# Dividing the second head's exponentials of each pair on GpSimd instead of VectorE

## The chip, the cores and the metric

The kernel runs on one core of a Trainium2 chip, with inputs and output in the chip's main memory. The metric is the device time of one execution in microseconds (us). Before the change it is 2291.26 us, the median of 3 runs (2284.45 to 2292.47).

## The reference

The input x is 4 x 1024 x 1024 in fp32. It is normalised, and two branches are computed from it: attention with 16 heads of 64 columns in 4 groups that share keys and values, with a sliding window of 512 and 4 sink positions, and a small network on the last row of each batch whose result is gated with the input.

```python
xn = _layernorm(x, axis=-1)
# attention
att = jnp.einsum('bkgqd,bkjd->bkgqj', q, k) * scale
att = jnp.where(mask[None, None, None, :, :], att, -jnp.inf)
att = jax.nn.softmax(att, axis=-1)
y = jnp.einsum('bkgqj,bkjd->bkgqd', att, v)
s = y @ Wo.T
# network: thought from the last row, 4 steps of a layer norm and a gelu network
out = x + sigmoid(x @ gate_w + gate_b) * broadcast
g = _silu(layer_norm(out, out_gamma, out_beta))
return x + s * g
```

What matters here is the softmax: the exponentials of a row of scores are divided by their sum before they are multiplied with the values. All products run in fp32, the larger ones as sums of high and low parts.

## The kernel before

The program has two parts. `attend` makes the projections and the attention of all four batches, and stores y to memory; `finish` makes the gate, the output projection and the final norm, tile by tile. The change touches `attend` alone.

`attend` goes through 4 batches of 32 steps. A step s is one unit u = 32 b + s: one group of 4 heads (s // 8) and one block of 128 queries (qb = s % 8). A unit looks at 1 to 5 blocks of 128 keys, and for qb above 4 at 4 sink columns too, so a row of `probs` is 128, 256, 384, 512, 640 or 644 columns wide. Of the 32 units of a batch, 12 have 644 columns. `probs` has 8 slots: 4 heads of this unit and 4 of the one before.

Every engine has its order written out by hand in its own `step(b, s)`; semaphores tie them together.

- TensorE makes the scores of heads 0 and 1 (L1010), then the first two transpositions of unit u - 1's probabilities (`turn_probs`, L1039, four heads of one key block at a time), then whatever the step holds of other work: a tile of the next batch turned (L928), rows of the small network (L858), then the scores of heads 2 and 3, further transpositions, pieces of the projections (L973), and last the product with the values (`values`, L1075) of unit u - 1, sinks last. `turn_probs(u, 0)` waits until all four heads are divided.
- VectorE adds the mask and finds the maximum, one head at a time (L1286), splits projections and turned tiles in high and low parts (L1258, L1274), adds the network's sums (L1346). At the end of a step it takes the reciprocal of a pair's two sums (`invert`, L1294), divides these two heads (`divide`, L1303), copies the turned sinks of unit u - 1 (`take_sinks`, L1320), and does the second pair. In steps 21 to 28 of the first three batches it also takes statistics of a tile of the next batch (L86, L90) before the first pair, and normalises the tile (L105) after the second. In steps 26 to 31 of the last batch it splits one or two pieces of the gate's weights there (L1422, two inputs from SBUF). The next step begins with the copy of y (L1310), which TensorE needs before it may use that bank again.
- ScalarE makes the exponentials with their sums (L768) and copies the transpositions from PSUM (L759).
- GpSimd has little to do. In its own loop over the steps it finds 1 / standard deviation of the tile that VectorE has statistics of (`ln_rstd`: an add L96 and a power L98), issues the load of a tile of x (`load_x`, L645, steps 20 to 27 of the first three batches), fills in sink columns of k and v (steps 2, 8 and 27), and for units with sinks packs the divided sink columns of the four heads (`pack_sinks`, L677).
- SyncE issues nearly all other transfers.

The pair's reciprocal is what the divisions wait for:

```python
dve.wait_ge(exp_done, GROUP * u + 2 * pair + 2)
dve.reciprocal(inv_sum[:, part], row_sum[:, part]).then_inc(inv_ready, 1)
```

Of the kernel before, what the change touches and what calls it, by code (L numbers as in the profile page):

```python
# [22 lines left out]
ALU = mybir.AluOpType  # L23
AX = mybir.AxisListType

P = 128
B, T, C = 4, 1024, 1024
HEADS, KV, HS = 16, 4, 64
WINDOW, SINK = 512, 4
HID = 4096  # L30
KB = C // P
TB = T // P
# [11 lines left out]
GROUP = HEADS // KV  # L44
UNITS = KV * TB
# [23 lines left out]
def blocks_of(qb):  # L69

    return min(qb + 1, WB + 1)
# [36 lines left out]
def unit_of(s):  # L108


    return s // TB, s % TB
# [7 lines left out]
def has_sink(qb):  # L119
    return qb > WB  # L120
# [30 lines left out]
def packed_before(u):  # L151

    return (TB - WB - 1) * (u // TB) + max(0, u % TB - WB - 1)
# [12 lines left out]
def attend(nc, shared, y_stored, WT, Y, BC, XS, x, gate_w, Wq, Wk, Wv, in_gamma, in_beta, agg_w, agg_b, pn_gamma, pn_beta, d1_w, d1_b, d2_w, d2_b,  # L166
           bc_w, bc_b):

    with ExitStack() as ctx:
        def sb(name, shape, dt=F32):  # L170
            return ctx.enter_context(nc.sbuf_tensor(name, shape, dt))
# [4 lines left out]
        def sem(name):  # L176
            return ctx.enter_context(nc.semaphore(name))
# [13 lines left out]
        probs = sb("probs", [P, 2 * GROUP, WIDTH])  # L191
# [5 lines left out]
        neg_max, row_sum, inv_sum = (sb(n, [P, 2 * GROUP]) for n in ("neg_max", "row_sum", "inv_sum"))  # L197
# [59 lines left out]
        x_full, x_high, x_taken = sem("x_full"), sem("x_high"), sem("x_taken")  # L257

        scores_ready, masked, exp_done = sem("scores_ready"), sem("masked"), sem("exp_done")
        inv_ready, normed = sem("inv_ready"), sem("normed")  # L260
        turned, pt_ready, pv_done, y_ready = sem("turned"), sem("pt_ready"), sem("pv_done"), sem("y_ready")

        fw_used, rows_ready, f_turned = sem("fw_used"), sem("rows_ready"), sem("f_turned")
# [160 lines left out]
        def v_parts(b, t):  # L424

            return v[:, 0:2 + b % 2:1 + b % 2, t, :, :]
# [9 lines left out]
        with nc.Block() as block:  # L436
# [166 lines left out]
            def _(pool):  # L603
# [60 lines left out]
                def v_sinks(b):  # L664
# [3 lines left out]
                    for head in range(GROUP):  # L668
                        pool.dma_start(v_sink[SINK * head:SINK * head + SINK, :, :].rearrange("p (m g) d -> p m g d", g=2),
                                       v_parts(b, 0)[0:SINK]).then_inc(v_sink_ready, 16)  # L670

                def pack_sinks(u):
                    slots = slice(GROUP * (u % 2), GROUP * (u % 2) + GROUP)
                    pool.wait_ge(normed, GROUP * u + GROUP)
                    if u >= 2:
                        pool.wait_ge(turned, turns_before(u - 1))
                    pool.tensor_copy(sink_cols[u % 2][:, :, :], probs[:, slots, WIDE:WIDE + SINK]  # L677
                                     ).then_inc(sinks_packed, 1)
# [12 lines left out]
                for b in range(B):  # L691
                    for s in range(UNITS):
                        if s == 0 and b:
                            thought_rstd(b)
                        if s == 2:
                            v_sinks(b)
                        if s == 8:
                            k_sinks(b, 1)
                        if b + 1 < B:
                            if s == 27:  # L700
                                k_sinks(b + 1, 0)
                            if 0 <= s - TURN0 + 1 < TB:
                                x_rstd(b + 1, s - TURN0 + 1)
                            if 0 <= s - TURN0 + 2 < TB:
                                load_x(b + 1, s - TURN0 + 2)
                        if has_sink(unit_of(s)[1]):
                            pack_sinks(UNITS * b + s)

# [131 lines left out]
            def _(pe):  # L840
# [180 lines left out]
                def turn_probs(u, i):  # L1021
                    qb = u % TB
                    if i == 0:
                        pe.wait_ge(normed, GROUP * u + GROUP)
                    if turns_before(u) + i >= 2:
                        wait_taken(*(turn_two_ago(u, i)))

                    for step_no in (u, u + 1):
                        item = turned_in(*divmod(step_no, UNITS))
                        if item and (step_no == u or i >= 2):  # L1030
                            pe.wait_ge(x_taken, 2 * turned_no(item) + 2)
                    if i == blocks_of(qb):
                        pe.wait_ge(sinks_packed, packed_before(u) + 1)
                        pe.transpose(t_ps[(turns_before(u) + i) % 2][0:SINKS, 0:P],
                                     sink_cols[u % 2][:, :, :].rearrange("p h k -> p (h k)"), ident[:, :]
                                     ).then_inc(turned, 1)
                        return
                    for head in range(GROUP):
                        last = pe.transpose(t_ps[(turns_before(u) + i) % 2][:, bass.ts(head, P)],  # L1039
                                            probs[:, GROUP * (u % 2) + head, P * i:P * i + P], ident[:, :])  # L1040
                    last.then_inc(turned, 1)
# [146 lines left out]
            def _(dve):  # L1188
# [107 lines left out]
                def divide(b, s, head):  # L1296
                    _, qb = unit_of(s)
                    u = UNITS * b + s
                    width = blocks_of(qb) * P + (SINK if has_sink(qb) else 0)
                    slot = GROUP * (u % 2) + head  # L1300
                    if head % 2 == 0:
                        dve.wait_ge(inv_ready, 2 * u + head // 2 + 1)
                    dve.tensor_scalar(probs[:, slot, 0:width], probs[:, slot, 0:width], inv_sum[:, slot:slot + 1], None,  # L1303
                                      ALU.mult).then_inc(normed, 1)

# [55 lines left out]
                def step(b, s):  # L1361
                    u = UNITS * b + s
                    found = places(b, s)
                    ahead = s - TURN0 + 1 if b + 1 < B and 0 <= s - TURN0 + 1 < TB else None

                    def take_place(i):
                        if found[i] and found[i][4] == STEPS:
                            take_low(*found[i][:3])

                    if u >= 2:  # L1370
                        take_y(u - 2)
                    mask_scores(b, s, 0)
                    mask_scores(b, s, 1)
                    if b and s == 0:
                        if b == 1:
                            dve.wait_ge(bias_loaded, 32)
                        add_rows(b, thought, thought)
                        think(b)
                    if b and s == 1:
                        scale_cols(2, 1 + b)  # L1380
                    if turned_in(b, s):
                        for half in range(2):
                            turned_low(u, turned_in(b, s), half)
                    take_place(0)
                    if b == B - 1 and s == FOLD_AT:
                        add_rows(B, thought, thought)
                        dve.wait_ge(thought_ready, 2 + 2 * B)
                        dve.tensor_copy(t_rows, thought).then_inc(t_rows_ready, 1)
                    if b == B - 1 and s == TURN_AT:
                        dve.wait_ge(f_turned, 2 + B)  # L1390
                        dve.tensor_copy(cols_view[:, 0:KB, :], f_cols.rearrange("p (k b) -> p k b", b=B)
                                        ).then_inc(cols_ready, 1)
                    if b == B - 1 and s == BC_FOLD_AT:
                        dve.wait_ge(bias_loaded, 48)
                        add_rows(1 + B, t_rows, None)
                    if s in HIDDEN_AT[b]:
                        add_hidden(b, HIDDEN_AT[b][s])
                    if TILES_AT[b][s]:
                        add_sums(b, s)
                    mask_scores(b, s, 2)  # L1400
                    mask_scores(b, s, 3)
                    if ahead is not None:
                        stats(b + 1, ahead)
                    invert(b, s, 0)
                    divide(b, s, 0)
                    divide(b, s, 1)
                    take_place(1)
                    if u and has_sink((u - 1) % TB):
                        take_sinks(u - 1)
                    invert(b, s, 1)  # L1410
                    divide(b, s, 2)
                    divide(b, s, 3)
                    if ahead is not None:
                        normalise(b + 1, ahead)
                    if b and s == 0:
                        apply_thought(b)
                    take_place(2)
                    take_place(3)
                    if b == B - 1:
                        for k in GATE_AT.get(s, ()):  # L1420
                            dve.wait_ge(gate_high, k + 1)
                            dve.tensor_tensor(x_lo[:, k, :], xn[k % 2], x_hi[:, k, :].bitcast(F32),  # L1422
                                              ALU.subtract).then_inc(gate_split, 1)
# [393 lines left out]
```

## Time and profile before

| | |
|---|---|
| median of 3 runs | 2291.26 us (2284.45 to 2292.47) |
| the profiled execution, its own time | 2282.0 us |
| its span, first to last instruction | 2280.3 us |
| mean granted TensorE clock | 0.993 |
| busy: TensorE, VectorE, ScalarE, GpSimd | 2207.4, 1456.2, 857.6, 150.6 us |

The attention takes the span to about 1557 us, `finish` the rest. A row of the timeline gives the start in us from the span's start, the duration in us, the engine (PE is TensorE, PEld its weight load, DVE VectorE, ACT ScalarE, POOL GpSimd), the line of the kernel, the operation, what it writes and reads, its shapes and how many instructions are merged in the row; in brackets the idle time before it and what ended it. A row of groups gives the busy time in us, the mean of one in ns, and the idle time before them.

### The profile page before, as it was taken

Reading aid. Unit: us, or ns where it says so; the run is one execution under the profiler, and the core shown is the slowest. Engines: PE = TensorE matmul, PEld = TensorE weight load, DVE = VectorE, ACT = ScalarE, POOL = GpSimd, SP = SyncE. Lnnn points to the kernel's source line nnn. Section 1 sums busy time; section 2 is a strip of 40 time slices with the busy share of each in tenths; the row PEclk is TensorE's granted clock in tenths of the full one; section 3 lists DMA queues with packets and bytes.
Section 4 is the critical chain, followed back from the end, with each engine's and each line's share of the span. In section 5 each row is a group of like instructions: output and inputs, shape, how many; then the busy total and the mean of one; then the engine's idle time right before and its main releaser. Section 6 shows DMA issues by size and latency. Waiting matters only on the chain. (4 is left out here: it accounts for less than half of the span.)

```text
span 2280.3 us, 35897 instructions
## 1 busy us (share of the span) xinstructions
PE 2207.4 (97%) x13577; PEld 1626.1 (71%) x13577; DVE 1456.2 (64%) x3071; ACT 857.6 (38%) x1837; POOL 150.6 (7%) x367
## 2 busy tenths in 40 slices
PE   7999999999999999999999999988999999999998
PEld 6666666766666676666676766656888888888886
DVE  7555567555666746566665556575766776667667
ACT  2354554444454435455443545463111111111111
POOL 2000001000001100000100000000010100100100
PEclk9999999999999999999999999999999999999999
DMA  7586459533447734435863354555243342342431
GB/s 253 176 253 191 139 178 282 188 106 109 157 153 231 244 115 144 160 122 171 276 200 108 117 196 144 211 176 192 93 147 120 119 147 98 141 146 93 147 119 66
DMA packets 173357, 366.53 MB, mean 161 GB/s; under 512 B 12424, under 2 KB 110856, under 8 KB 158880
## 3 DMA queue, kind: packets, MB, share of 16 engines
q1 hardware_dynamic: 168240, 348.30, 45.9%
q0 software_dynamic: 4544, 14.75, 1.9%
q8 instruction: 91, 1.49, 0.3%
q10 hardware_dynamic: 432, 1.57, 0.2%
q14 instruction: 50, 0.41, 0.1%
HBM read 284.79 MB, written 79.72 MB: 160 GB/s over the span
## 5 line engine op out<-in xcount | busy, mean ns | idle before, releaser
L759 ACT ACTIVATE pt<-t_ps 128x512 f32<-128x512 f32 x480 | 265.9, 595 | 533.5 <-PE t_ps L1039 531.8
L973 PE MATMUL j_ps<-x_hi,w 128*128 128x512 f32 x1232 | 413.5, 404 | 0.0
L768 ACT ACTIVATE probs<-probs,neg_max 128x644 f32<-128x644 f32 (+5 forms) x512 | 352.8, 694 | 57.6 <-DVE neg_max L1286 57.4
L1286 DVE CUSTOM_DVE_ANT_0 probs<-s_ps,mask 128x644 f32<-128x644 f32 (+5 forms) x512 | 316.5, 656 | 80.9 <-PE s_ps L1010 76.3
L1672 PE MATMUL out_ps<-wo,w 128*128 128x512 f32 x1536 | 355.1, 390 | 2.7 <-DVE w L1729 2.7
L1672 PEld LDWEIGHTS out_ps<-wo,w 128*128 128x128 f32 x1536 | 289.4, 188 | 63.3 <-issue 3.1
L1672 PE MATMUL gate_ps<-x_hi,w 128*128 128x512 f32 x1024 | 280.9, 391 | 4.8 <-PEq L436 4.8
L1039 PE MATMUL t_ps<-ident,probs 128*128 128x128 f32 x1920 | 270.0, 279 | 10.5 <-ACT pt L759 4.7
L973 PEld LDWEIGHTS j_ps<-x_hi,w 128*128 128x128 f32 x1232 | 230.8, 189 | 53.0 <-issue 6.3
L1010 PEld LDWEIGHTS s_ps<-k_hi,q 64*128 64x128 f32 x1536 | 146.1, 185 | 171.4 <-issue 97.3
L1010 PE MATMUL s_ps<-k_hi,q 64*128 64x512 f32 (+4 forms) x1536 | 243.6, 351 | 10.0 <-DVE q L1258 5.7
L1039 PEld LDWEIGHTS t_ps<-ident,probs 128*128 128x128 f32 x1920 | 208.2, 141 | 51.2 <-issue 19.6
L973 PE MATMUL j_ps<-x_lo,w 128*128 128x512 f32 x616 | 244.3, 397 | 0.0
L1075 PE MATMUL o_ps<-pt,v 128*64 128x256 f32 x1920 | 237.0, 388 | 1.6 <-DVE small_rows L1218 1.5
L1672 PEld LDWEIGHTS gate_ps<-x_hi,w 128*128 128x128 f32 x1024 | 192.6, 189 | 45.0 <-issue 5.2
L1303 DVE TENSOR_SCALAR probs<-probs,inv_sum 128x644 f32<-128x644 f32 (+5 forms) x512 | 218.0, 468 | 9.1
L1075 PEld LDWEIGHTS o_ps<-pt,v 128*64 128x64 f32 x1920 | 127.4, 137 | 93.9 <-issue 41.6
L1659 ACT ACTIVATE b_res<-b_a 128x1024 f32<-128x1024 f32 x32 | 33.9, 1061 | 424.3 <-DVE b_a L1759 424.3
L1672 PE MATMUL gate_ps<-x_lo,w 128*128 128x512 f32 x512 | 158.1, 390 | 0.0
L858 PE MATMUL o_ps<-fw,cols 128*32 128x512 f32 x1088 | 141.9, 606 | 5.4 <-issue 2.8
L973 PEld LDWEIGHTS j_ps<-x_lo,w 128*128 128x128 f32 x616 | 117.1, 190 | 21.5
L1010 PE MATMUL s_ps<-k_lo,q 64*128 64x512 f32 (+4 forms) x768 | 128.6, 327 | 0.0
(177 smaller groups left out, 2182.9 us busy)
## 6 DMA issues: line engine op xcount, KB each, us to landing
fw<-in_L_ffn_d_w_dram SPq DMA_DIRECT2D x128, 1024.0 KB, 5.2
w<-WT SPq DMA_DIRECT2D x36, 1024.0 KB, 5.1
w<-XS SPq DMA_DIRECT2D x64, 512.0 KB, 6.4
XS<-x_hi SPq DMA_DIRECT2D x32, 512.0 KB, 8.0
XS<-x_lo SPq DMA_DIRECT2D x32, 512.0 KB, 9.4
Y<-y SPq DMA_DIRECT2D x256, 64.0 KB, 2.3
b_x<-in_L_attn_x_dram SPq DMA_DIRECT2D x32, 512.0 KB, 4.2
b_y<-Y SPq DMA_DIRECT2D x32, 512.0 KB, 6.5
```

Source lines behind the costliest of these rows:

```text
L759: act.activation(pt[:, m % PT_SLOTS, :, :], bank[:, :].rearrange("p (h q) -> p h q", q=P), ACT.Copy).then_inc(pt_ready, 1)
L768: act.activation(probs[:, slot, 0:width], probs[:, slot, 0:width], ACT.Exp, bias=neg_max[:, slot:slot + 1], scale=-1.0, accum_out=row_sum[ ...
L858: last = pe.matmul(f_ps[COLS * j:COLS * j + COLS, :], cols[:, B * first[j]:B * first[j] + COLS], fw[n % 2][:, bass.ts(j, BANK)], start=sta ...
L973: last = pe.matmul(bank_of((kind, b, n)), w[:, slot, wp * C + c * P:wp * C + c * P + P], xs[:, c, bass.ts(ch, BANK)], start=i == 0, stop=i ...
L1010: last = pe.matmul(s_ps[head][:, o:o + width], qs[h, pair, bass.ts(qb, P)], k[h, g // 2, blocks, 0:keys], start=m == 0, stop=m == 2)
L1039: last = pe.transpose(t_ps[(turns_before(u) + i) % 2][:, bass.ts(head, P)], probs[:, GROUP * (u % 2) + head, P * i:P * i + P], ident[:, :])
L1075: last = pe.matmul(o_ps[HS * half:HS * half + HS, 0:2 * P], lhs, rhs[:, half::2, :], start=i == 0, stop=i == turns_of(qb) - 1)
L1286: dve.tensor_tensor_reduce(out=probs[:, slot, 0:width], in0=s_ps[head % 2][:, 0:width], in1=m, scale=-SCALE, scalar=-NEG, op0=ALU.add, op1 ...
L1303: dve.tensor_scalar(probs[:, slot, 0:width], probs[:, slot, 0:width], inv_sum[:, slot:slot + 1], None, ALU.mult).then_inc(normed, 1)
L1659: act.activation(res[:, :], a[:, :], ACT.Sigmoid).then_inc(sig2_ready, 1)
L1672: last = pe.matmul(out_[:, bass.ts(half, BANK)], lhs[:, c, :], rhs(c, half), start=(c == 0 and lhs is hi and rhs is w_hi), stop=(c == KB - ...
```

## The change

Of each pair of heads VectorE divides the first, GpSimd the second, both after the same reciprocal. The divisions of VectorE count in `normed`, those of GpSimd in a new semaphore `normed_second`, and who waited for four divisions in one now waits for two in each. In GpSimd's loop the divisions stand last in a step, before `pack_sinks`.

```diff
+                def divide_second(u, pair):
+                    width = blocks_of(u % TB) * P + (SINK if has_sink(u % TB) else 0)
+                    slot = GROUP * (u % 2) + 2 * pair + 1
+                    pool.wait_ge(inv_ready, 2 * u + pair + 1)
+                    pool.tensor_scalar(probs[:, slot, 0:width], probs[:, slot, 0:width], inv_sum[:, slot:slot + 1], None,
+                                       ALU.mult).then_inc(normed_second, 1)
+
                 def pack_sinks(u):
                     slots = slice(GROUP * (u % 2), GROUP * (u % 2) + GROUP)
-                    pool.wait_ge(normed, GROUP * u + GROUP)
+                    pool.wait_ge(normed, 2 * u + 2)
+                    pool.wait_ge(normed_second, 2 * u + 2)
...
                                 load_x(b + 1, s - TURN0 + 2)
+                        for pair in range(2):
+                            divide_second(UNITS * b + s, pair)
                         if has_sink(unit_of(s)[1]):
                             pack_sinks(UNITS * b + s)
...
                 def turn_probs(u, i):
                     qb = u % TB
                     if i == 0:
-                        pe.wait_ge(normed, GROUP * u + GROUP)
+                        pe.wait_ge(normed, 2 * u + 2)
+                        pe.wait_ge(normed_second, 2 * u + 2)
...
                     slot = GROUP * (u % 2) + head
-                    if head % 2 == 0:
-                        dve.wait_ge(inv_ready, 2 * u + head // 2 + 1)
+                    dve.wait_ge(inv_ready, 2 * u + head // 2 + 1)
...
                     invert(b, s, 0)
                     divide(b, s, 0)
-                    divide(b, s, 1)
                     take_place(1)
                     if u and has_sink((u - 1) % TB):
                         take_sinks(u - 1)
                     invert(b, s, 1)
                     divide(b, s, 2)
-                    divide(b, s, 3)
```

## Rows read from the trace of the kernel before

**Rows 1.** The page, busy time of each engine with its share.

```profile
PE 2207.4 (97%) x13577; PEld 1626.1 (71%) x13577; DVE 1456.2 (64%) x3071; ACT 857.6 (38%) x1837; POOL 150.6 (7%) x367
```

**Rows 2.** The waits of TensorE: us in total, times, longest.

```profile
PE o_ps L1075 <- DVE small_rows L1320: 5.1, 6, 0.8
...
PE t_ps L1039 <- DVE probs L1303: 1.6, 3, 0.9
```

**Rows 3.** Timeline, batch 1, step 19 (unit 51).

```profile
668.17 0.89 DVE L1303 TENSOR_SCALAR probs<-probs,inv_sum 128x512 f32<-128x512 f32 x2
...
669.84 1.09 PE L1039 MATMUL t_ps<-ident,probs 128*128 128x128 f32 x8
```

**Rows 4.** Groups of VectorE's divisions, shapes kept apart: the widest, the narrowest.

```profile
L1303 DVE TENSOR_SCALAR probs<-probs,inv_sum 128x644 f32<-128x644 f32 x192 | 98.0, 553 | 3.4
...
L1303 DVE TENSOR_SCALAR probs<-probs,inv_sum 128x128 f32<-128x128 f32 x64 | 15.5, 284 | 1.1
```

**Rows 5.** Groups of GpSimd, shapes kept apart.

```profile
L98 POOL TENSOR_TENSOR b_rstd<-b_rstd,b_minus_half 128x1 f32<-128x1 f32 x64 | 35.1, 549 | 5.0
...
L614 POOL MEMSET mask<- 128x644 f32 x1 | 0.6, 637 | 0.0
...
L618 POOL TENSOR_SCALAR_AFFINE_SELECT mask<-mask 128x128 f32<-128x128 f32 x2 | 0.6, 290 | 0.2 <-POOL mask L615 0.2
...
L626 POOL TENSOR_SCALAR_AFFINE_SELECT own_head<-own_head 16x4 f32<-16x4 f32 x1 | 0.2, 184 | 0.1
```

**Rows 6.** All of GpSimd's sink copies, by line: ns min/median/max.

```profile
L677 POOL COPY sink_cols<-probs x48: 190/197/1129, 139.7 to 1550.3; 128x16 f32<-128x16 f32 x48
```

**Rows 7.** Timeline, last batch, step 29.

```profile
1528.77 2.35 DVE L1422 TENSOR_TENSOR x_lo<-xn,x_hi 128x1024 fp32r<-128x1024 f32 x2
...
1528.92 1.12 POOL L677 COPY sink_cols<-probs 128x16 f32<-128x16 f32 x1 [57.61 <-DVE probs L1303]
```

**Rows 8.** Timeline, batch 1, step 22.

```profile
705.07 0.11 DVE L1294 RECIPROCAL inv_sum<-row_sum 128x2 f32<-128x2 f32 x1
705.21 1.02 DVE L1303 TENSOR_SCALAR probs<-probs,inv_sum 128x644 f32<-128x644 f32 x2
705.24 0.18 POOL L96 TENSOR_TENSOR rstd<-mv,eps_x 128x1 f32<-128x1 f32 x1 [11.64 <-DVE mv L90]
...
706.16 0.60 POOL L645 DMA_DIRECT2D xn<-in_L_attn_x_dram  x1
706.26 0.68 DVE L1320 TENSOR_TENSOR small_rows<-t_ps,own_head 16x512 f32<-16x512 f32 x1
...
708.12 0.81 DVE L105 TENSOR_SCALAR xn<-xn,mv,rstd 128x1024 f32<-128x1024 f32 x1
...
708.76 1.09 PE L1039 MATMUL t_ps<-ident,probs 128*128 128x128 f32 x8
```

**Rows 9.** The same of step 23.

```profile
717.53 0.11 DVE L1294 RECIPROCAL inv_sum<-row_sum 128x2 f32<-128x2 f32 x1
...
720.73 1.09 PE L1039 MATMUL t_ps<-ident,probs 128*128 128x128 f32 x8
```

**Rows 10.** The same of step 26.

```profile
756.71 0.75 DVE L1303 TENSOR_SCALAR probs<-probs,inv_sum 128x384 f32<-128x384 f32 x2
...
757.52 0.60 POOL L645 DMA_DIRECT2D xn<-in_L_attn_x_dram  x1
...
758.81 1.09 PE L1039 MATMUL t_ps<-ident,probs 128*128 128x128 f32 x8
```

**Rows 11.** The same of step 27.

```profile
769.85 0.73 POOL L645 DMA_DIRECT2D xn<-in_L_attn_x_dram  x1
...
771.97 1.09 PE L1039 MATMUL t_ps<-ident,probs 128*128 128x128 f32 x8
```

**Rows 12.** Timeline, last batch, from step 29 into step 30.

```profile
1527.63 0.17 DVE L1294 RECIPROCAL inv_sum<-row_sum 128x2 f32<-128x2 f32 x1 [1.09 <-ACT probs L768]
...
1531.51 1.92 PE L858 MATMUL o_ps<-fw,cols 128*32 128x512 f32 x16 [1.28 <-DVE y L1310]
```

More of the change, by code:

```diff
@@ L259, in attend @@
         scores_ready, masked, exp_done = sem("scores_ready"), sem("masked"), sem("exp_done")
-        inv_ready, normed = sem("inv_ready"), sem("normed")
+        inv_ready, normed, normed_second = sem("inv_ready"), sem("normed"), sem("normed_second")
         turned, pt_ready, pv_done, y_ready = sem("turned"), sem("pt_ready"), sem("pv_done"), sem("y_ready")
```

## The prediction

> **What bounds the kernel now.** I read the busy line of the page, then the waits of TensorE, then the timeline of single steps. TensorE is busy for 97% of the span [rows 1], so an edit can only bring time where TensorE visibly stands still, and costs time wherever its next input comes too late. The waits show which of its stalls VectorE's work around the change ends: the largest are 5.1 us in 6 waits for the turned sinks, and the divided exponentials themselves are waited for 1.6 us in 3 waits [rows 2]. That is 6.7 us, most of what a lighter VectorE could give. Against the 64% of VectorE [rows 1] this is the first thing to see: VectorE has much work but is seldom what TensorE waits for.
>
> The number that decides is the slack: the time from the last division of a unit to the first transposition that reads it. In an ordinary step it is comfortable: in unit 51 the last pair's divisions run from 668.17 for 0.89 us and TensorE comes at 669.84, 0.78 us after [rows 3]. This is among the smallest of the steps without a tile of the next batch; nearly all others have more. It is smaller in steps 22, 23, 26 and 27 of the first three batches, where the next batch's tiles are normalised, and in steps 26 to 31 of the last batch.
>
> **What is removed.** VectorE loses 256 of 512 divisions. A wide one takes 553 ns, a 128-column one 284 ns [rows 4], so (553 - 284) / 516 = 0.52 ns a column. Half of the 192 wide ones alone is 96 x 0.553 = 53 us, and with the narrower ones (32 of each of five widths, 284 ns and up) it is some 110 us. I cost it at almost no gain: by rows 1 and 2 the cover is TensorE's own work. Only what follows a removed division on VectorE and ends a stall could come earlier, the sinks.
>
> **What is added.** GpSimd runs 256 tensor_scalar over up to 644 columns. The trace has none on GpSimd. Its nearest relatives are the mask selections, also one input and one output: 290 ns for 128 columns, 184 ns for 4 [rows 5], so 0.86 ns a column over 0.18 us. That gives 0.74 us for 644, 0.63 for 512, 0.51 for 384 columns. Lower end: a fill of 644 columns that reads nothing takes 637 ns [rows 5]. Upper end: the costliest fixed part of a GpSimd operation here, the power at 549 ns for one column [rows 5], with the same 0.56 us of columns, 1.11 us. I take 0.74 us, from the rows nearest in kind. Two waits on the semaphores move from one counter to two and no engine is asked more than a compare for that; the pack of the sinks has 5 further transpositions' time before TensorE needs it: nothing.
>
> **The shared port.** GpSimd and VectorE hinder each other here. The sink copy of 16 columns takes 197 ns in the median, but up to 1129 ns, and that one starts 0.15 us after a subtraction of two SBUF tensors began on VectorE and ends about when the first of the two does; the second does not hold it any longer [rows 6, 7]. So I let a long operation of either engine wait for the other's, and a waiting one go in between two of the other's. A waiting one loses some 0.04 us. The Trainium skill, page "SBUF — State Buffer", section "SBUF: two separate sides", says more: whichever starts first holds the pair for the whole instruction, and the other fully blocks. The trace agrees only for longer operations: the one-column add at 705.24 lasts its usual 0.18 us beside a division that began at 705.21 [rows 8]. By the rule each division would wait in full, which is also what my sum has; by the small add alone it would not.
>
> So the last GpSimd division of a pair ends at the reciprocal's start + 0.20 + 0.55 (VectorE's own) + 0.04 + 0.74 = 1.53 us, in place of 0.20 + 1.02 = 1.22 us: 0.3 us later at 644 columns, 0.28 us at 512 (1.37 for 1.09). At upper-end times it is 0.7 us later, still within the 0.78 us of rows 3. So the ordinary steps cost nothing.
>
> **Steps 22 and 23 (three batches).** GpSimd has its other work ahead of the divisions: the two rstd operations and the descriptors of the next x load, which start at 706.16 and take 0.60, so it is free at 706.76 [rows 8]. VectorE divides head 0 from 705.21 to 705.76, does the sinks (0.68) 0.5 us earlier than before, and the second reciprocal, and asks for the port for head 2 at about 706.67. It is a near race. If VectorE wins: head 2 until 707.22, GpSimd's head 1 until 708.02, then the normalisation of 0.81 us that has been waiting on VectorE, then head 3 from 708.9 to 709.66. TensorE wanted it at 708.76 [rows 8]: 0.9 us. If GpSimd wins: 706.76 + 0.74 + 0.04 + 0.55 + 0.04 + 0.74 = 708.9, 0.15 us. Middle 0.5 us. Step 23 has the same distances from its reciprocal at 717.53, but TensorE comes at 720.73 [rows 9], 0.49 us sooner by that measure: 1.0 us.
>
> **Steps 26 and 27.** In step 26 GpSimd is free at 757.52 + 0.60 = 758.12. VectorE has by then done its two 0.42 us divisions (from 756.71) and started the normalisation (0.81) at about 757.8, so the two divisions of 0.51 us start after 758.6 and end at 759.7, where TensorE wants them at 758.81 [rows 10]: 0.9 us. Step 27: free at 769.85 + 0.73 = 770.58, normalisation until 771.0, then 2 x 0.63 and two gaps: 772.35 against 771.97 [rows 11], 0.4 us. Steps 21, 24, 25 and 28 have slack enough. Sum per batch 0.5 + 1.0 + 0.9 + 0.4 = 2.8 us, three batches 8.4 us.
>
> **The last batch, steps 26 to 31.** Here VectorE is close to being the bound: behind the last division stand one or two splits of the gate (1.22 us each, two SBUF inputs), then the copy of y that TensorE waits for with 1.28 us [rows 7, 12]. Before, the splits began 1.14 us after the reciprocal's start (1527.63 to 1528.77). After, they wait for GpSimd's head 3: 0.20 + 0.55 + 0.04 + 0.74 + 0.04 = 1.57 us, so 0.4 us later, and y with them. The saved division is thus more than given back by the wait for the port. Six steps: 0.3 (384 columns), 0.1 (there VectorE idles after), then 4 of about 0.4: 2.0 us.
>
> The x loads, on GpSimd's queue, stand before the divisions in each step and wait for an early transposition of that step, so they go out as before. The output half of the kernel is unchanged.
>
> **Sum.** 8.4 + 2.0 = +10.4 us, no gain set against it, as the earlier sinks end in the later transposition of the same step. The profiled execution took 2282.0 us and would take 2292.4. The three runs have a median of 2291.3, 9.3 us above it, so against them I expect 2301. Bounds: with 0.64 us a wide division each term falls by 0.1 or 0.2: about +7. With 1.11 us, 0.37 us is added twice in each of the 12 steps and once in each of 6: 8.9 + 2.2, so about +21.5. About 0.5% (11.5 us) is what a measurement can tell from no change; the forecast's own range, 2298 to 2313, lies across it.
>
> **Rivals.** *GpSimd is slow (slower).* Its loop takes twice the time a column of the mask selections, 1.72 ns: 1.3 us for 644, 1.06 for 512, 0.84 for 384 columns. In steps 22 and 23 twice 0.56 us is added, in 26 twice 0.33, in 27 twice 0.43: 2.8 + 1.1 + 1.1 + 0.7 + 0.9 = 6.6 us a batch, and 0.5 us more in each of the last six: 20 + 5 = +25 us, 2316. It decides from about 0.8 us a wide division. For: no row has a wide GpSimd arithmetic operation. Against: both selection and fill walk at under 0.9 ns. The Trainium skill, "GPSIMD Engine Reference", section "Elementwise — side-by-side cycle accounting", measures about 2.6 cycles an element for two inputs, an estimated 1.4 us for 644 columns and more than that in the sum; its section "Engine selection" has one input at roughly line rate, which would leave my sum.
>
> *The port hinders less (no change).* If divisions overlap freely, step 22 gains up to 0.5 us, step 23 and 27 nothing, step 26 loses 0.4 us: within 2 us, 2291. For: the small add. Against: rows 6 and 7.
>
> *VectorE's queue was the hidden bound (faster).* All 6.7 us of rows 2 come back and up to as much again behind TensorE's modelled ends: 2278 to 2285. For: VectorE is 110 us lighter. Against: TensorE's 97%, and the 1.6 us only that it waits for divisions.
>
> *The change is empty in effect*, because GpSimd comes so late everywhere that nothing overlaps: this is the slow case and has no chance of its own.
>
> **Chances.** Forecast 0.62, of it 0.34 within 0.5% and 0.28 above; port hinders less 0.13; slow GpSimd 0.17; faster 0.08. Faster 0.08, same 0.47, slower 0.45. The range leaves out the faster case and the far end of the slow one: 2285 to 2317.
>
> **What would show it.** GpSimd's divisions near 0.74 us at 644 columns when alone, a few hundred ns more beside VectorE; the transposition's wait for GpSimd's division visible in steps 22, 23, 26, 27 and at most there; unit 51's like untouched; the gate splits some 0.4 us later after the reciprocal; the output half equal. I am wrong if wide GpSimd divisions take over 1.2 us, if VectorE's divisions stretch in ordinary steps so that TensorE waits there too, or if TensorE's stalls shrink in steps 22 and 23.

## The result, and the profile after

| | before | after |
|---|---|---|
| median of 4 runs | 2291.86 us (2284.45 to 2292.48) | 2352.39 us (2349.5 to 2353.71) |
| the profiled execution, its span | 2282.0, 2280.3 us | 2352.68, 2351.0 us |
| mean granted TensorE clock | 0.993 | 0.977 |

The kernel is slower by a ratio of 1.0281 (in brackets, here and below, the 95% interval: [1.0262, 1.03]), some 60 us; the forecast was 2301, its range ended at 2317. The two profiled spans lie 70.7 us apart, as the profiled execution of before is a quick one of its four. All ratios are of executions in the chip's usual, faster state; one of the 12 of the sinks-first kernel below ran at a granted clock of 0.555 and took 3587.96 us. The page's busy line after the change, to be held against [rows 1]:

```profile
PE 2237.1 (95%) x13577; PEld 1648.3 (70%) x13577; DVE 1387.0 (59%) x2815; ACT 857.9 (36%) x1837; POOL 591.6 (25%) x623
```

VectorE lost 69 us of busy time, not the 110 of the prediction: its 256 divisions are busy for 138.5 us where the 512 were for 218.0, since some stretch beside GpSimd's. GpSimd gained 441 us, and TensorE is 30 us busier with the same 13577 matmuls: some of them ran longer. GpSimd's new work, by form (busy us, mean ns | idle before):

```profile
L677 POOL TENSOR_SCALAR probs<-probs,inv_sum 128x644 f32<-128x644 f32 x96 | 216.5, 2256 | 306.8 <-DVE inv_sum L1306 305.9
...
L677 POOL TENSOR_SCALAR probs<-probs,inv_sum 128x512 f32<-128x512 f32 x32 | 58.0, 1817 | 75.0 <-DVE inv_sum L1306 74.8
...
L677 POOL TENSOR_SCALAR probs<-probs,inv_sum 128x128 f32<-128x128 f32 x32 | 25.0, 781 | 109.1 <-DVE inv_sum L1306 108.9
```

A wide division takes 2256 ns on GpSimd; VectorE took 553 [rows 4], and the prediction assumed 740. The waits of TensorE (us in total, times, longest):

```profile
PE t_ps L1051 <- issue: 50.7, 30, 3.9
...
PE o_ps L1087 <- DVE small_rows L1331: 1.8, 6, 0.4
```

The sinks are waited for 1.8 us where it was 5.1 [rows 2], as a lighter VectorE should give. ("Sinks" are the turned probabilities of the 4 sink columns, `small_rows`.) But the first transposition of the probabilities now waits 50.7 us in 30 waits. "Issue" says that the profile names no releaser; the timeline names it by the times. Batch 1, step 22, the step of [rows 8]:

```profile
729.34 0.11 DVE L1306 RECIPROCAL inv_sum<-row_sum 128x2 f32<-128x2 f32 x1
...
730.44 0.64 POOL L646 DMA_DIRECT2D xn<-in_L_attn_x_dram  x1
...
731.00 0.70 DVE L1314 TENSOR_SCALAR probs<-probs,inv_sum 128x644 f32<-128x644 f32 x1
731.12 4.32 POOL L677 TENSOR_SCALAR probs<-probs,inv_sum 128x644 f32<-128x644 f32 x2
731.61 1.38 DVE L105 TENSOR_SCALAR xn<-xn,mv,rstd 128x1024 f32<-128x1024 f32 x1
735.54 1.56 PE L1051 MATMUL t_ps<-ident,probs 128*128 128x128 f32 x8 [2.89 <-issue]
...
751.80 1.94 PE L1051 MATMUL t_ps<-ident,probs 128*128 128x128 f32 x8 [3.90 <-issue]
```

VectorE is done with its two heads at 731.70. GpSimd, after the two small rstd operations, issues the x load's descriptors until 731.08, although the reciprocal has been ready since 729.45, then divides both heads one after the other until 735.44, and TensorE starts 0.1 us later after 2.89 us of standing still. Its eight transpositions then take 1.56 us in place of 1.09 [rows 8]. In step 23, 16 us on, the same happens and they take 1.94 (the last row). The windows of after say why (columns: window, its length, then busy us of PE, PEld, DVE, ACT and POOL with the instruction count, the mean granted clock as a share of full speed, DMA share, GB/s):

```profile
730.00:735.00 5.00, 2.27 (x21) 1.19 (x16) 4.72 (x10) 0.00 (x0) 4.96 (x4) 1.00 1.09 339
735.00:740.00 5.00, 4.46 (x28) 2.98 (x32) 0.12 (x1) 3.46 (x8) 0.64 (x2) 0.66 0.28 95
...
750.00:755.00 5.00, 3.20 (x15) 2.85 (x16) 0.70 (x5) 1.82 (x6) 1.90 (x2) 0.50 0.52 180
```

In the window after step 22's stall the granted clock is 0.66 in the mean: part of it ran at full speed (2.4 GHz), part at the lower level (1.2 GHz, a share of 0.50). The window around the end of step 23's stall ran at the lower level throughout. In the four such windows of before (705 to 725) it is 1.00 throughout.

Where is the time lost? The delay of after against before, read at the first transposition of the same unit, was 24.3 us at the start of step 22 of batch 1 (720.57 against 696.29) and 40.8 us in step 29 (842.83 against 802.08). The rows, before first:

```profile
696.29 1.09 PE L1039 MATMUL t_ps<-ident,probs 128*128 128x128 f32 x8
...
802.08 1.09 PE L1039 MATMUL t_ps<-ident,probs 128*128 128x128 f32 x8
```

```profile
720.57 1.09 PE L1051 MATMUL t_ps<-ident,probs 128*128 128x128 f32 x8
...
842.83 1.09 PE L1051 MATMUL t_ps<-ident,probs 128*128 128x128 f32 x8
```

The same difference, taken at each step's first reciprocal, shows how much each step loses, a fallen clock included (us):

| step | 22 | 23 | 24, 25 | 26 | 27 | 28 | 29 to 31 | 22 to 31 together |
|---|---|---|---|---|---|---|---|---|
| batch 1 | 3.5 | 4.3 | 0.4 | 3.4 | 3.5 | 1.3 | 0.1 | 16.5 |
| last batch | 0.4 | 1.1 | 0.1 | 3.2 | 5.2 | 1.6 | 0.3 | 11.9 |

Batches 0 and 2 lose 17.9 and 17.8 in the same steps. These four stretches make 64 of the 70.7 us between the two spans; 3 of the rest arise in the very first steps, and the output part gives under 1.

The last batch loses by another mixture. In its step 26 TensorE waited 3.26 us:

```profile
1558.12 4.01 POOL L677 TENSOR_SCALAR probs<-probs,inv_sum 128x384 f32<-128x384 f32 x2 [8.08 <-DVE inv_sum L1306]
...
1559.79 1.23 DVE L1431 TENSOR_TENSOR x_lo<-xn,x_hi 128x1024 fp32r<-128x1024 f32 x1 [0.33 <-ACT x_hi L815]
...
1562.22 1.94 PE L1051 MATMUL t_ps<-ident,probs 128*128 128x128 f32 x8 [3.26 <-issue]
```

The second of the two divisions starts about when VectorE begins a split of the gate's weights, and takes 2.32 us, where the mean of the 384-column divisions is 1.44.

### The profile page after: what moved, and what is told of

Its sections match the earlier page's. It is cut to its first block and busy times, and to the rows that moved or that the text cites. A ratio compares the mean times of both kernels' runs of the same rounds, so it can differ in the third digit from the quotient of the medians.

```text
span 2351.0 us, 35930 instructions
## 1 busy us (share of the span) xinstructions
PE 2237.1 (95%) x13577; PEld 1648.3 (70%) x13577; DVE 1387.0 (59%) x2815; ACT 857.9 (36%) x1837; POOL 591.6 (25%) x623
## 5 line engine op out<-in xcount | busy, mean ns | idle before, releaser
L677 POOL TENSOR_SCALAR probs<-probs,inv_sum 128x644 f32<-128x644 f32 (+5 forms) x256 | 445.8, 1746 | 755.3 <-DVE inv_sum L1306 753.6
L1051 PE MATMUL t_ps<-ident,probs 128*128 128x128 f32 x1920 | 277.1, 285 | 58.2 <-issue 50.7
L1051 PEld LDWEIGHTS t_ps<-ident,probs 128*128 128x128 f32 x1920 | 214.3, 144 | 99.6 <-issue 72.6
L96 POOL TENSOR_TENSOR b_rstd<-b_mv,b_eps_x 128x1 f32<-128x1 f32 x32 | 26.1, 814 | 491.2 <-DVE b_mv L90 491.2
L1314 DVE TENSOR_SCALAR probs<-probs,inv_sum 128x644 f32<-128x644 f32 (+5 forms) x256 | 138.5, 541 | 9.1
```

The source lines that it names most:

```text
L677: pool.tensor_scalar(probs[:, slot, 0:width], probs[:, slot, 0:width], inv_sum[:, slot:slot + 1], None, ALU.mult).then_inc(normed_second, 1)
```

## The experiments

The theory at this point: GpSimd's division is three times as dear as assumed, all of the loss comes from the few steps with small slack, and part of it is the clock. The rivals: GpSimd is slow only because VectorE holds the shared port; the loss is spread over all steps; the two extra waits cost something by themselves.

**VectorE's relief alone.** The second heads stay undivided, and GpSimd only counts.

```diff
-                    pool.tensor_scalar(probs[:, slot, 0:width], probs[:, slot, 0:width], inv_sum[:, slot:slot + 1], None,
-                                       ALU.mult).then_inc(normed_second, 1)
+                    pool.sem_inc(normed_second, 1)
```

> This kernel leaves the second head of each pair undivided: VectorE is lighter as in the change, and GpSimd does nothing for it. Theory A (the loss is GpSimd's division coming late, and a lighter VectorE is worth next to nothing): 2284 to 2292 us, within 0.3% of the kernel before. Rival (VectorE's queue was a hidden bound and the change only hides that gain): under 2275 us.

Measured: 2277.96 against 2286.74 us, ratio 0.9955 [0.9937, 0.9973]. The two waits for sinks and divided exponentials:

```profile
PE o_ps L1086 <- DVE small_rows L1330: 2.2, 6, 0.4
...
PE t_ps L1050 <- DVE probs L1313: 0.6, 1, 0.6
```

They fell by 3.9 us together; the time fell by 0.45%, 10 us, to between the two bands expected. So the relief was worth more than the prediction granted ("almost no gain"), though the waits shown account for less than half of it and no run here locates the rest. The new waits cost nothing that shows. All of the loss is GpSimd's.

**Only where there is slack.** GpSimd divides in 105 of the 128 units; in the 23 others (steps 22, 23, 26, 27, 28 of every batch, and 29 to 31 of the last) VectorE has all four heads, as before.

```diff
-                            divide_second(UNITS * b + s, pair)
+                            if not is_tight(UNITS * b + s):
+                                divide_second(UNITS * b + s, pair)
...
                     divide(b, s, 0)
+                    if is_tight(u):
+                        divide(b, s, 1)
```

> GpSimd divides the second heads in all steps but 22, 23, 26, 27, 28 (and 29 to 31 in the last batch), where VectorE divides all four; these are 23 of 128 units. Theory A (all of the loss lies where the slack was under 1.5 us): within 5 us of the kernel before, about 2292 us, though 105 of 128 units still use GpSimd. Rival (a cost spread over all steps, such as the shared port slowing VectorE everywhere): most of the 60 us stays, over 2320 us.

Measured: 2287.89 against 2286.74 us, ratio 1.0008 [0.9998, 1.0018].

```profile
PE o_ps L1105 <- DVE small_rows L1349: 5.0, 6, 0.8
...
PE t_ps L1069 <- issue: 1.6, 6, 0.3
```

GpSimd's division is as dear here (2261 ns for 644 columns), 210 of the 256 are made, and it costs at most 0.2%. Nearly the whole loss sits in 23 units. The gain of VectorE's relief isn't to be had in the others either: the sinks are waited for 5.0 us, as before, so that wait too belongs to the tight steps.

**The price of the operation, three ways.** First a constant in place of the factor read per row (the second heads are halved, not normalised), and a copy in place (they stay as they are):

```diff
-                    pool.tensor_scalar(probs[:, slot, 0:width], probs[:, slot, 0:width], inv_sum[:, slot:slot + 1], None,
+                    pool.tensor_scalar(probs[:, slot, 0:width], probs[:, slot, 0:width], 0.5, None,
```

> GpSimd multiplies by a constant instead of the row's inverse sum, so the second heads are not normalised; all else as in the change. If the per-row factor read from memory makes the operation slow, it falls from 2.2 us to about 0.75 us at 644 columns and the time to about 2300 us. If the walk over the columns is what costs (theory A: 2.9 ns a column for any one-input arithmetic), it stays within 0.2 us of 2.2 us and the time near 2352 us.

```diff
+                    pool.tensor_copy(probs[:, slot, 0:width], probs[:, slot, 0:width]).then_inc(normed_second, 1)
```

> GpSimd copies the second heads in place instead of dividing them, so they are not normalised; same width and same waits. If any GpSimd operation over 644 columns takes 2 us, the copy does too and the time stays near 2350 us. If it is the multiplication (theory A: the walk of this operation alone is slow, as mask selections and short copies go at about 1 ns a column), the copy takes about 1.0 us and the time is about 2300 us, the figure of the prediction's sum.

Measured, one run each: 2340.21 us with the constant (before: 2286.74 in that comparison), 2292.31 with the copy (before: 2289.19). The groups with the constant:

```profile
L677 POOL TENSOR_SCALAR probs<-probs 128x644 f32<-128x644 f32 x96 | 196.2, 2046 | 325.0 <-DVE inv_sum L1306 323.7
...
L677 POOL TENSOR_SCALAR probs<-probs 128x128 f32<-128x128 f32 x32 | 19.2, 601 | 113.4 <-DVE inv_sum L1306 113.3
```

and with the copy:

```profile
L1313 DVE TENSOR_SCALAR probs<-probs,inv_sum 128x644 f32<-128x644 f32 x96 | 104.8, 1092 | 3.4
L677 POOL COPY probs<-probs 128x644 f32<-128x644 f32 x96 | 69.3, 726 | 418.2 <-DVE inv_sum L1305 418.2
...
L677 POOL COPY probs<-probs 128x128 f32<-128x128 f32 x32 | 9.4, 294 | 119.7 <-DVE inv_sum L1305 119.7
```

The copy costs (726 - 294) / 516 = 0.84 ns a column, just the price that the prediction took for the division, and with it the kernel would have been 3 us slower than before. This is the prediction's own price, built: its sum said +10, and 2300 us was expected of this run. So at its own price the sum put the waits too high, by some 7 us as far as one run can tell. The multiplication, with whichever factor, has (2046 - 601) / 516 = 2.8 ns a column. The per-row factor adds 0.2 us to an instruction of either width.

**One engine after the other.** GpSimd starts when VectorE has divided its head, so that it has no division beside it.

```diff
-                    pool.wait_ge(inv_ready, 2 * u + pair + 1)
+                    pool.wait_ge(normed, 2 * u + pair + 1)
```

> GpSimd waits for VectorE's division of the pair's first head instead of the reciprocal, so the two no longer start together. If the port is what stretches GpSimd's division (rival B: 0.75 us of its own, the rest waiting), it falls to under 1.2 us at 644 columns where nothing else is beside it, and the time falls below 2340 us. Theory A (2.1 us or more of its own): the duration falls by no more than 0.5 us, and the later start costs as much or more: 2350 to 2362 us.

Measured: 2359.87 us, ratio 1.0318 [1.0296, 1.0339]. Groups, then one step's timeline:

```profile
L677 POOL TENSOR_SCALAR probs<-probs,inv_sum 128x644 f32<-128x644 f32 x96 | 191.1, 1991 | 340.8 <-DVE probs L1314 340.4
...
L677 POOL TENSOR_SCALAR probs<-probs,inv_sum 128x128 f32<-128x128 f32 x32 | 22.5, 702 | 113.4 <-DVE probs L1314 113.3
```

```profile
139.95 0.56 DVE L1314 TENSOR_SCALAR probs<-probs,inv_sum 128x644 f32<-128x644 f32 x1
140.61 1.90 POOL L677 TENSOR_SCALAR probs<-probs,inv_sum 128x644 f32<-128x644 f32 x1 [8.61 <-DVE probs L1314]
```

Started after VectorE's division, GpSimd still needs 1.90 us for 644 columns. That is the median of the 96, as 0.60 us is of those with 128 columns; the means of the groups are higher because in a few steps later work of VectorE runs beside. So a column costs (1.90 - 0.60) / 516 = 2.5 ns, and the rival "it is only the port" falls: of 2.26 us 1.90 are GpSimd's own, and 0.36 comes on top when a VectorE division starts with it. Serialised, the kernel is slower still.

**The clock.** Before the wait in steps 22, 23, 26 and 27 of the first three batches TensorE makes 14 to 26 needless transpositions, into the bank that the real one overwrites next; its two waits for the divisions move behind them.

```diff
+                    if i == 0:
+                        if u < UNITS * (B - 1):
+                            for _ in range({22: 20, 23: 26, 26: 15, 27: 14}.get(u % UNITS, 0)):
+                                pe.transpose(t_ps[turns_before(u) % 2][:, 0:P], ident[:, :], ident[:, :])
+                        pe.wait_ge(normed, 2 * u + 2)
+                        pe.wait_ge(normed_second, 2 * u + 2)
```

> As the change, but TensorE makes 14 to 26 needless transpositions of the identity while it waits in steps 22, 23, 26 and 27 of the first three batches. Theory: a part of the loss, some 12 to 15 us, is TensorE's clock, which falls to half after stalls of 3 us (0.50 to 0.66 granted in the 5 us behind two of them); with the wait filled the clock stays up and the time falls to about 2338 us. Rival (the clock reading follows the stall and costs nothing more): 2350 to 2356 us.

Measured: 2329.45 us, ratio 1.0193 [1.0168, 1.0219], where 2338 was expected; the mean granted clock is 0.993, as before the change. Step 23 of batch 1 and its two windows:

```profile
736.36 4.64 POOL L677 TENSOR_SCALAR probs<-probs,inv_sum 128x644 f32<-128x644 f32 x2
...
737.12 3.06 PE L1044 MATMUL t_ps<-ident 128*128 128x128 f32 x26
...
741.14 1.07 PE L1054 MATMUL t_ps<-ident,probs 128*128 128x128 f32 x8 [0.96 <-POOL probs L677]
```

```profile
735.00:740.00 5.00, 4.63 (x44) 3.59 (x40) 4.89 (x10) 0.16 (x2) 4.93 (x4) 1.00 1.08 337
740.00:745.00 5.00, 3.74 (x32) 2.26 (x30) 0.83 (x2) 2.82 (x8) 1.19 (x2) 1.00 0.33 112
```

GpSimd is just as late, but the clock stays at full speed and the transpositions take 1.07 us. Work that produces nothing makes the kernel 0.9% faster than it is after the change: some 20 us of the loss went with it. By steps 22 to 31 of the traces it is 21.3 us, of which 18.0 fall in the three batches with fills. GpSimd's divisions are no reason for that share: in the 15 steps 22, 23, 26, 27 and 28 of these batches the last one ends 80.6 us after the step's first reciprocal in all, against 80.9 without the fills. It is the clock's. The other 3.3 are in the last batch, which has none; there, in step 26, VectorE's split happened to start after GpSimd's division instead of beside it (the row of this run below has 2.79 us, against 4.01 in the change), so they are not all clock. And with less idle time the profile does name the releaser, GpSimd's division.

```profile
1535.32 2.79 POOL L677 TENSOR_SCALAR probs<-probs,inv_sum 128x384 f32<-128x384 f32 x2 [8.07 <-DVE inv_sum L1309]
```

**The load behind the divisions.** In GpSimd's loop the x load moves behind the two divisions.

```diff
-                            if 0 <= s - TURN0 + 2 < TB:
-                                load_x(b + 1, s - TURN0 + 2)
                         for pair in range(2):
                             divide_second(UNITS * b + s, pair)
+                        if b + 1 < B:
+                            if 0 <= s - TURN0 + 2 < TB:
+                                load_x(b + 1, s - TURN0 + 2)
```

> As the change, but GpSimd issues the load of the next x tile after its divisions instead of ahead of them. Theory: in steps 22, 23, 26 and 27 GpSimd starts its first division only after 0.6 us of this issue, and each of the 12 steps gets that back: 8 us, and a little of the clock, so 2340 to 2345 us. Rival (the issue is hidden, as GpSimd waits for the reciprocal anyway): 2350 to 2354 us. If the later load comes too late for its statistics, over 2355 us.

Measured: 2334.03 us, ratio 1.0199 [1.0179, 1.0218], 18 us better than the change where 8 and a little of the clock were expected (2340 to 2345). Step 23 of batch 1:

```profile
736.93 4.31 POOL L677 TENSOR_SCALAR probs<-probs,inv_sum 128x644 f32<-128x644 f32 x2
737.45 0.62 DVE L1315 TENSOR_SCALAR probs<-probs,inv_sum 128x644 f32<-128x644 f32 x1
737.99 0.80 DVE L105 TENSOR_SCALAR xn<-xn,mv,rstd 128x1024 f32<-128x1024 f32 x1
741.19 0.64 POOL L646 DMA_DIRECT2D xn<-in_L_attn_x_dram  x1
...
741.34 1.94 PE L1052 MATMUL t_ps<-ident,probs 128*128 128x128 f32 x8 [2.94 <-issue]
```

The stall here is 2.94 us where it was 3.90, and the mean granted clock 0.984 where it was 0.977, so part of the 18 may be clock. The two edits together, with shorter fills, tell the shares apart:

```diff
+                            for _ in range({22: 16, 23: 20, 26: 10, 27: 9}.get(u % UNITS, 0)):
```

> The change with both edits: the wait of TensorE filled with needless transpositions (9 to 20) and the x load issued after GpSimd's divisions. If clock and queue order are separate parts of the loss, with the order itself worth 8 us (12 times 0.65) and the clock the rest of its 18 us: 2329 - 8 = about 2321 us. If the order's 18 us were all its own: 2311 us.

Measured: 2323.78 us, ratio 1.0168 [1.0151, 1.0185]. Against the filled waits alone (1.0193) the order brings 0.25%, 6 us; the other 12 of its 18 were the clock, close to the 2321 us that this split of the shares gave. What stays, 1.68% or 38 us, is mostly the division that ends too late.

**A quarter instead of half.** GpSimd divides head 1 alone; head 3 goes back to VectorE.

```diff
-                        for pair in range(2):
-                            divide_second(UNITS * b + s, pair)
+                        divide_second(UNITS * b + s, 0)
...
                     divide(b, s, 2)
+                    divide(b, s, 3)
```

> GpSimd divides only the second head of the first pair, VectorE the other three. Theory A, with 2.25 us a wide division: it ends in time nearly everywhere; step 22 loses 0.3 us, 23 and 26 0.75 us each, 27 0.45 us, three times: 7 us, and the last batch nothing, so about 2296 to 2300 us. Rival (port contention spread over all steps): half of the 62 us, about 2320 us.

Measured: 2303.75 us, ratio 1.0071 [1.005, 1.0092]: +16 us where +7 was expected (2296 to 2300). TensorE's wait and step 23 of batch 1 say why:

```profile
PE t_ps L1050 <- DVE probs L1313: 11.1, 9, 1.8
```

```profile
729.17 2.71 DVE L1313 TENSOR_SCALAR probs<-probs,inv_sum 128x644 f32<-128x644 f32 x2
729.29 2.25 POOL L677 TENSOR_SCALAR probs<-probs,inv_sum 128x644 f32<-128x644 f32 x1
...
731.94 1.09 PE L1050 MATMUL t_ps<-ident,probs 128*128 128x128 f32 x8 [1.82 <-DVE probs L1313]
```

GpSimd's division ends at 731.54, early enough to cost 1.5 us of stall at most. But VectorE's two divisions, 1.1 us of work, take 2.71: the first takes 1.80 and the second ends 0.34 us after GpSimd's. Both were held beside GpSimd's division. Here the port costs, and TensorE waits for VectorE.

**Who else could help.** Two edits of the kernel before. In the first, ScalarE divides the second heads, in steps 22, 23, 26 and 27 of the first three batches alone:

```diff
+                    if on_act(u):
+                        for pair in range(2):
...
+                            act.wait_ge(inv_ready, 2 * u + pair + 1)
+                            act.activation(probs[:, slot, 0:width], probs[:, slot, 0:width], ACT.Copy,
+                                           scale=inv_sum[:, slot:slot + 1]).then_inc(normed_act, 1)
```

> The kernel before, but in steps 22, 23, 26 and 27 of the first three batches ScalarE divides the second head of each pair (a copy with the inverse sum as its scale), about 0.75 us at 644 columns and beside no port of VectorE. These are the steps where the slack was short and where leaving the second heads out gave up to 9 us. Theory: VectorE's sinks come 0.5 us earlier in steps 22 and 23 and the divisions end in time: 3 to 4 us a run faster, about 0.15%, at the edge of what can be told. If ScalarE's division is slower than that or its other copies come late: no change or up to 0.3% slower.

In the second, VectorE copies the sinks ahead of head 1, in the steps where no projection stands between the divisions and the sinks:

```diff
-                    divide(b, s, 1)
+                    if found[1]:
+                        divide(b, s, 1)
...
                         take_sinks(u - 1)
+                    if not found[1]:
+                        divide(b, s, 1)
```

> The kernel before, but VectorE copies the turned sinks ahead of the second division where no projection stands between. If the wait for the sinks (5.1 us in 6 waits) was worth what it shows, half of it comes back less what the later division costs in step 23: 1 to 2 us faster, under what can be told; if it is no change or slower, the gain of the half-left-out kernel came from elsewhere.

Measured: ScalarE 2282.22 against 2287.0 us, ratio 0.9984 [0.9972, 0.9996]; sinks first 2289.2, ratio 1.0 [0.9988, 1.0012]. The waits with ScalarE, and with the sinks first:

```profile
PE t_ps L1062 <- DVE probs L1326: 2.3, 4, 0.9
PE o_ps L1098 <- DVE small_rows L1343: 2.3, 6, 0.4
```

```profile
PE t_ps L1039 <- DVE probs L1303: 3.6, 6, 0.9
PE o_ps L1075 <- DVE small_rows L1320: 2.4, 6, 0.4
```

Sinks first halves the one wait and more than doubles the other [rows 2]: a queue reordered, nothing gained. So the sinks' wait was not the source of the 10 us either. ScalarE takes work away: the sinks' wait falls by 2.8 us while the wait for the divisions grows by 0.7, and this is the only kernel of those that divide all heads that beats the one before, by 0.16%, as expected. ScalarE's own division takes 833 ns for 644 columns, between VectorE's 553 and GpSimd's 2256:

```profile
L816 ACT ACTIVATE probs<-probs,inv_sum 128x644 f32<-128x644 f32 x12 | 10.0, 833 | 2.2 <-DVE inv_sum L1317 2.2
```

## Why the prediction was wrong

**The place held, and in three batches the mechanism.** It named the steps with little slack, 22, 23, 26 and 27 of three batches and 26 on of the last, with, in the first three, the x load's descriptors ahead of the divisions. All twelve lost time; of the last six, 26 to 28 bore it (10.0 us) and 29 to 31 lost 0.3. Not foreseen: step 28 ("slack enough", it lost 1.3 us), steps 22 and 23 of the last batch (1.5 us together), and unit 51, which was to be untouched and stood still for 0.27 us.

**In the last batch the mechanism failed.** The prediction had the gate splits wait for GpSimd, 0.4 us a step, and TensorE wait for the y behind them. In step 29 the splits began earlier after the pair's reciprocal than before (0.95 against 1.14 us), the two took 2.68 us for 2.35, and y came 0.15 us later. What cost time was again the division itself, wanted 1.0 to 1.5 us after the reciprocal: in steps 26 and 27 it ended 3.3 and 3.6 us after it, with the split beside GpSimd's division and stretching it to 2.32 and 2.47 us. In steps 29 to 31 TensorE waited for it too, 1.06 us in step 29, but then waited 0.34 us for y where it had waited 1.28 [rows 12], so that the steps lost next to nothing.

**The step that failed is the term "I take 0.74 us, from the rows nearest in kind".** It measured 2.26 us, and 1.90 without a VectorE division at its start; a column cost 2.5 ns in place of 0.86. A mask selection (one input, one output) and a fill (no input) are near in form but don't multiply; the copy walks at their pace, the multiplication at a third of it. The upper bound of 1.11 us took only the fixed part from a dear row and kept the cheap column. The trace showed no wide arithmetic on GpSimd at all; the one row of GpSimd arithmetic there, the power, takes 549 ns for a single column [rows 5], and nothing excluded a column price several times that of a copy. The rival that had this mechanism doubled the column, to 1.3 us, where it needed to be tripled, and so ended at 2316.

Put into the prediction's own sum, the measured price comes near, in part by luck. In step 22 and in 23 twice 1.5 us is added, in 26 twice 0.93 (384 columns, 1438 for 510 ns), in 27 twice 1.19 (512 columns, 1817 for 630): 10.2 a batch, 31 in three; in the last six 0.93 + 1.19 + 4 x 1.5 = 8.1. With the 10.4 this is +49 us. Filled waits, which keep the clock, measured 1.93%, 44 us. But the 10.4 was too high for its own price (the copy, in one run, lost 3 us), and the last batch, some 10 us in this sum and 11.9 measured, is spread wrongly: steps 26 and 27 would lose 2.5 us together and lost 8.4, steps 29 to 31 would lose 5.7 and lost 0.3.

**Missing in the sum: TensorE's clock.** No term stood for it. With stalls of 2 to 4 us every 16 us the granted clock fell to its lower level after them, worth 18 to 20 us (2352 against 2329).

**"Almost no gain" was half right.** VectorE's relief is worth 10 us where nothing takes its place, and the 5.1 us of [rows 2] did shrink, to 1.8. The rival that gave all of it back had 2278 to 2285 and would have been right with an engine that costs nothing: the ratio 0.9955 makes 2281 of the 2291 before. It was the other term of the sum that buried it.

**The port.** The prediction let each long operation wait for the other's; the runs disagree among themselves. For it: with the copy, VectorE's division takes 1092 ns for 553; with one head of four the second ends only after GpSimd's; in the change the normalisation of step 22 takes 1.38 us for 0.81; in step 26 of the last batch a split of two SBUF inputs stretches GpSimd's division. Against it: in ordinary steps VectorE's division, begun 0.06 us ahead of GpSimd's, keeps its 556 ns and GpSimd's loses only 0.36 of them; in step 23 with the load behind, VectorE's division and its normalisation run for 0.62 and 0.80 us, hardly longer than alone [rows 4, 8], wholly inside a GpSimd division. The rule of the Trainium skill, "SBUF — State Buffer", section "SBUF: two separate sides", that the second fully blocks (of a GpSimd operation and a VectorE one in a 2-port mode or with two SBUF inputs), fits the cases for it and not those against. What decides it stays open; none of the runs varied the distance of the two starts by itself. For the verdict it matters little, since GpSimd's own 1.9 us decide.

Of the two rules weighed on the price, the Trainium skill's "GPSIMD Engine Reference", section "Engine selection", (one input at roughly line rate) holds for the copy and fails for the division; the 2.6 cycles an element of its section "Elementwise — side-by-side cycle accounting", given for two inputs, were the nearer, an estimated 1.4 us against 1.90 measured. To give that case 0.17 was too little.

## What to carry to other kernels

Price an operation moved to another engine by a row of the same arithmetic on that engine; where there is none, the price per column is unknown too, and a copy or a fill is its lower bound, not its middle. Before moving work off a busy engine, list the steps where its result is wanted within the new duration: here 18% of the units bore nearly all of the loss, and the engine that had a moment free in just those steps (ScalarE) was worth more than the one with most idle time. A stall of some us costs more than itself, since the matmuls after it may run at the lower clock: compare the duration of the same eight transpositions, 1.09 and 1.94 us.

## What the runs showed of the hardware that was not expected

- GpSimd's multiplication by a per-row factor takes 0.60 us for 128 and 1.90 us for 644 columns in fp32 with no VectorE division beside it, a copy 0.29 and 0.73.
- A factor read from memory per row costs GpSimd about 0.2 us an instruction over a constant (2256 against 2046 ns at 644 columns, 781 against 601 at 128).
- Needless transpositions in a wait, 75 in each of three batches, kept the granted clock at 0.993; 18 to 20 us were won.
- GpSimd's descriptors (0.64 us for a tile of x) sit in the same queue as its arithmetic: put behind the divisions they won 18 us, of which 6 were the queue and the rest the clock.
